# Second attention's query norms computed in its normalising pass, weights turned in the second feed-forward, normalising shared by three engines

## The reference, cut to what matters

```python
def _layernorm(x, axis=-1, eps=1e-05):
    m = jnp.mean(x, axis=axis, keepdims=True)
    v = jnp.var(x, axis=axis, keepdims=True)
    return (x - m) / jnp.sqrt(v + eps)
...
# second attention: H = 16 heads of 8, top_u = 51 of 256 queries per head
Q, K, V = proj(Wq, bq), proj(Wk, bk), proj(Wv, bv)
query_norms = jnp.linalg.norm(Q, axis=2)
_, top_idx = jax.lax.top_k(query_norms, top_u)
Q_sel = jnp.take_along_axis(Q, top_idx[:, :, None], axis=1)
...
x = x + 0.5 * _L0_ffn_ref(_layernorm(x), ...)
x = x + _L0_attn_ref(_layernorm(x), ...)
x = x + 0.5 * _L0_ffn_ref(_layernorm(x), ...)
x = x + 0.5 * _L1_ffn_ref(_layernorm(x), ...)
x = x + _L1_attn_ref(_layernorm(x), ...)
x = x + 0.5 * _L1_ffn_ref(_layernorm(x), ...)
```

## Time and profile before

| | us |
|---|---|
| median of three runs | 1415.3 |
| the profiled execution | 1417.87 |
| its span | 1415.0 |
| busy: PE, DVE, ACT, POOL | 1165.7, 1143.2, 898.3, 695.7 |
| normalising pass before stage 2, first transpose to last copy | 316.65 to 326.13 |
| the same, stage 3, with its statistics | 385.49 to 400.63 |
| second feed-forward | 326.1 to 382.5 |
| second attention: query norms alone | 797.0 to 813.2 |
| second attention: seven rounds | 813.6 to 823.0 |

### The profile page before, as it was taken

How to read it: one execution, slowest core, us unless ns; L and a number is a source line. 1 busy time by engine, 2 the same in 40 slices (tenths; PEclk the granted TensorE clock), 3 DMA queues, 4 the chain that set the end, 5 groups by cost and what they waited for, 6 DMA issues and landing times.

```text
span 1415.0 us, 58469 instructions
## 1 busy us (share of the span) xinstructions
PE 1165.7 (82%) x22908; PEld 956.5 (68%) x22908; DVE 1143.2 (81%) x4087; ACT 898.3 (63%) x2094; POOL 695.7 (49%) x597
## 2 busy tenths in 40 slices
PE   1775898976648899999998759999668999999996
PEld 1563666655527788888888547777437888888886
DVE  4885888857889899999994378888689899999980
ACT  1762566647647878778784426666457687787871
POOL 2305445413037777778775300000058787788772
PEclk9896999987959999999999979999769999999999
DMA  6000000000002222112222000000002121222122
GB/s 167 8 0 1 2 0 0 0 1 1 0 0 48 47 57 46 44 44 46 58 44 48 1 0 1 0 0 0 1 16 53 41 59 44 44 48 56 44 59 78
DMA packets 27515, 42.86 MB, mean 30 GB/s; under 512 B 6960, under 2 KB 18480, under 8 KB 27440
## 3 DMA queue, kind: packets, MB, share of 16 engines
q1 hardware_dynamic: 27440, 41.82, 12.8%
HBM read 6.15 MB, written 2.10 MB: 6 GB/s over the span
## 4 chain that ended last, share of the span: by engine, by line
PE 43%; DVE 23%; ACT 10%; issue 10%; POOL 5%; DMA 4%; SPq 3%; DVEq 1%; ACTq 0%; POOLq 0%; PEldq 0%
PE bank L1715 12%; ACT work L1031 4%; POOL work L345 4%; DVE work L891 4%; DMA rowsD<-work 4%; PE bank L1697 4%; DVE work L934 4%; SPq L315 3%; PE bank L1405 3%; PE bank L1598 2%; DVE xn L565 2%; ACT L1197 2%; PE bank L1688 2%; PE bank L1418 2%; PE bank L1317 2%
## 5 line engine op out<-in xcount | busy, mean ns | idle before, releaser
L1715 PEld LDWEIGHTS bank<-rowsD,work 128*32 128x32 f32 x16384 | 360.6, 195 | 90.4 <-issue 89.7
L1715 PE MATMUL bank<-rowsD,work 128*32 128x32 f32 x16384 | 371.2, 274 | 56.1 <-DMA rowsD<-work 39.6
L422 POOL TENSOR_SCALAR work<-work 128x1024 f32<-128x1024 f32 x64 | 185.2, 2893 | 135.0 <-ACT work L1202 135.0
L409 POOL TENSOR_TENSOR work<-work 128x512 f32<-128x512 f32 x128 | 161.2, 1281 | 41.7 <-ACT work L1230 27.9
L1230 ACT ACTIVATE work<-bank 128x512 f32<-128x512 f32 x128 | 74.9, 612 | 153.8 <-PE bank L1715 150.5
L1202 ACT ACTIVATE work<-work 128x128 f32<-128x128 f32 x512 | 161.1, 405 | 4.1 <-DVE work L954 4.1
L1211 ACT ACTIVATE work<-work 128x128 f32<-128x128 f32 x512 | 160.2, 413 | 0.0
L424 POOL TENSOR_TENSOR work<-work 128x1024 f32<-128x1024 f32 x64 | 157.2, 2456 | 5.3
L934 DVE STREAM_TRANSPOSE work<-work 128x1024 f32<-128x1024 f32 x128 | 151.4, 1222 | 0.0
L1726 PE MATMUL bank<-kout,work 128*128 128x128 f32 x1024 | 128.1, 278 | 3.0 <-POOL work L409 3.0
L1697 PE MATMUL bank<-xT,kinT 128*128 (+1 forms) x512 | 126.6, 392 | 2.6 <-ACT work L1221 2.6
(11 more groups left out here) (196 smaller groups left out, 2285.9 us busy)
## 6 DMA issues: line engine op xcount, KB each, us to landing
rowsD<-work SPq DMA_DIRECT2D x256, 128.0 KB, 2.4
x_sb<-in_L_attn_x_dram SPq DMA_DIRECT2D x8, 256.0 KB, 5.0
out_dram<-x_sb SPq DMA_DIRECT2D x4, 512.0 KB, 5.3
headsel<-in_c_headsel_dram SPq DMA_DIRECT2D x1, 512.0 KB, 5.3
work<-in_L_ffn_key_in_dram SPq DMA_DIRECT2D x1, 512.0 KB, 7.9
kout<-in_L_ffn_key_out_dram SPq DMA_DIRECT2D x4, 128.0 KB, 4.8
work<-in_L_ffn_keys_dram SPq DMA_DIRECT2D x1, 256.0 KB, 2.9
wqkv<-in_L_attn_W_qkv_dram SPq DMA_DIRECT2D x1, 192.0 KB, 5.3
```

The costliest lines, as they stand in the source:

```text
L409: last = nc.gpsimd.tensor_tensor(cg[:, par, :].rearrange("p (j t) -> p j t", j=NCH)[:, :, half * 64:half * 64 + 64], csb[:, par, 512 * hal ...
L422: nc.gpsimd.tensor_scalar(wmask, both, 1.0 - 5e-7, None, ALU.is_ge).then_inc(s["wm"], 1)
L1715: last = nc.tensor.matmul(bank[2 + half][k * NK:(k + 1) * NK, :] .rearrange("p (j t c) -> p t c j", j=NCH, t=16)[:, t % 16, :, :], xrows[: ...
```

## The change

Four edits, made together.

1. **Normalising on three engines.** Of a group's four columns VectorE now writes two, GpSimd the third and ScalarE the fourth, the last as `Identity(scale * x + bias)` with a new tile `shift = negmean * rstd` that VectorE computes first. TensorE waits for all three. GpSimd and ScalarE start when `shift` is written. All loops of the pass are unrolled.
2. **Weights turned in the second feed-forward.** The 16 transposes, the four copies and the 16 small matmuls move from stage 1 into the second feed-forward, one bank at a time: groups 2 to 5 of TensorE's program each take four transposes between project in and project out, groups 6 and 7 eight small matmuls each; VectorE copies a bank after each of its updates 0 to 3. `weff` is copied by ScalarE in the pass of stage 3. The second feed-forward's loops are unrolled.
3. **Query norms inside the pass of stage 4.** After each group's transposes TensorE projects the queries of the group before, 512 tokens at once; ScalarE squares them after its next copy. The sums over heads become 16 matmuls with 32 columns in four column groups, eight for each half of the sequences, into four groups of partitions. Squares of all sequences are kept (`squares`, over `E1` and `PT1`).
4. **Order in the second attention.** VectorE's memsets come before the rounds. GpSimd copies `xs1` for the first sequence before the bias row, and TensorE projects that sequence before the selection is turned.

```diff
             for k in range(STAGES):
-                s = pr
+                s, base = pr, k * NG
+                pool.wait_ge(s["nr"], k + 1)
+                for n in range(NG):
+                    pool.wait_ge(s["tr"], base + n + 1)
+                    pool.sem_inc(s_go, 1)
+                    c = n * GT + 2
+                    nc.gpsimd.tensor_scalar(xn[:, n % 2, 2, :], x_sb[:, c, :], negmean[:, c:c + 1], rstd[:, c:c + 1],
+                                            ALU.add, ALU.mult).then_inc(s["xp"], 1)
                 pool.wait_ge(s["tr"], 2 + (k + 1) * NG)
...
                 if k == 4:
+                    pool.wait_ge(s["ev"], 2 + (k + 1) * NG)
+                    nc.gpsimd.tensor_copy(xs1, xT[:, 0:SEQ]).then_inc(L1["xs"], 1)
                     add_row(bo_bc, L1["cb"])
...
+            def keep_weights(g):
+                dve.wait_ge(s_tw, g + 1)
+                if g == 0:
+                    nc.vector.tensor_copy(w1T[:, :, :].rearrange("p a b -> p (a b)"), bank[0][:, :]).then_inc(s_cw, 1)
+                if g == 1:
+                    nc.vector.tensor_copy(keysT, bank[1][:, :]).then_inc(s_cw, 1)
+                if g > 1:
+                    nc.vector.tensor_copy(kinT[:, :, :, 16 * (g - 2):16 * (g - 1)].rearrange("p j c i -> p i c j"),
+                                          bank[g - 2][:, :].rearrange("p (i c j) -> p i c j", c=4, j=NCH)).then_inc(s_cw, 1)
...
+                nc.vector.tensor_tensor(shift[:, :], negmean[:, :], rstd[:, :], ALU.mult).then_inc(s["nr"], 1)
...
-                    for t in range(GT):
+                    for t in range(2):
                         c = n * GT + t
...
+                else:
+                    for g in range(NG - 2):
+                        sums(g + 1, (g + 1) % 2)
+                        update(g, g % 2)
+                        if g < 4:
+                            keep_weights(g)
...
-                with act.Fori(0, NG // 2) as i:
-                    for par in range(2):
-                        n = 2 * i + par
-                        act.wait_ge(s["tr"], base + n + 3)
-                        nc.scalar.activation(xT[:, bass.ds(n * GW, GW)], bank[6 + par][:, :],
-                                             ACT.Copy).then_inc(s["ev"], 1)
+
+                def normalise(n):
+                    act.wait_ge(s["tr"], base + n + 1)
+                    act.sem_inc(s_go, 1)
+                    c = n * GT + 3
+                    nc.scalar.activation(xn[:, n % 2, 3, :], x_sb[:, c, :], ACT.Identity, bias=shift[:, c:c + 1],
+                                         scale=rstd[:, c:c + 1]).then_inc(s["xa"], 1)
+
+                def evacuate(n):
+                    act.wait_ge(s["tr"], base + n + 3)
+                    nc.scalar.activation(xT[:, n * GW:(n + 1) * GW], bank[6 + n % 2][:, :],
+                                         ACT.Copy).then_inc(s["ev"], 1)
+
+                def query_squares(n):
+                    act.wait_ge(L1["pq"], n + 1)
+                    nc.scalar.activation(squares[n // 4][:, 2 * n % 8:2 * n % 8 + 2, :].rearrange("p a b -> p (a b)"),
+                                         bank[n % 2][:, :], ACT.Square, bias=bqc[:, 0:1]).then_inc(L1["psq"], 1)
+
+                act.wait_ge(s["nr"], k + 1)
+                normalise(0)
+                normalise(1)
+                for n in range(NG):
+                    evacuate(n)
+                    if n + 2 < NG:
+                        normalise(n + 2)
+                    if k == 4 and n > 0:
+                        query_squares(n - 1)
+                    if k == 3 and n == 0:
+                        act.wait_ge(s_tw, 5)
+                        nc.scalar.activation(weff[:, :], bank[0][:, :], ACT.Copy).then_inc(s_cw, 1)
+                if k == 4:
+                    query_squares(NG - 1)
...
-            def turn_weights():
-                pe.wait_ge(s_w, 16 * NW)
+            def turn_weights(g):
+                if g == 0:
+                    pe.wait_ge(s_w, 16 * NW)
+                if g > 1:
+                    pe.wait_ge(s_cw, g - 1)
                 for i in range(4):
-                    c = slice(i * P, (i + 1) * P)
-                    nc.tensor.transpose(bank[1][:, c], w1nat[:, i, :], ident[:, :])
-                    nc.tensor.transpose(bank[2][:, c], keysn[:, i, :], ident[:, :])
-                    nc.tensor.transpose(bank[3][:, c], kinn[:, i, :], ident[:, :])
-                    last = nc.tensor.transpose(bank[4][:, c], kinn[:, 4 + i, :], ident[:, :])
-                last.then_inc(s_ps, 1)
-
-            def fold_keys():
-
-                pe.wait_ge(s_set, SET_KEYS)
+                    src = (w1nat[:, i, :], keysn[:, i, :], kinn[:, i, :], kinn[:, 4 + i, :])[g]
+                    last = nc.tensor.transpose(bank[g % 2][:, i * P:(i + 1) * P], src, ident[:, :])
+                last.then_inc(s_tw, 1)
+
+            def fold_keys(g):
+                if g == 0:
+                    pe.wait_ge(s_cw, 3)
...
-                        last = nc.tensor.matmul(bank[5][:, c * NK:(c + 1) * NK], wqn[:, c, :], kv[:, q, h, :],
-                                                start=True, stop=True)
-                last.then_inc(s_ps, 1)
-                pe.wait_ge(s_set, SET_ALL)
+                for c in range(4 * g, 4 * g + 4):
+                    last = nc.tensor.matmul(bank[0][:, c * NK:(c + 1) * NK], wqn[:, c, :], kv[:, c // PH, c % PH, :],
+                                            start=True, stop=True)
+                if g == 3:
+                    last.then_inc(s_tw, 1)
+
+            def query_squares(n):
+                if n == 5:
+                    head_norms(0)
+                pe.wait_ge(pr["ev"], 2 + 4 * NG + n + 1)
+                if n >= 2:
+                    pe.wait_ge(L1["psq"], n - 1)
+                nc.tensor.matmul(bank[n % 2][:, :], w1T[:, 0, :], xT[:, n * GW:(n + 1) * GW], start=True,
+                                 stop=True).then_inc(L1["pq"], 1)
+
+            def head_norms(half):
+                pe.wait_ge(L1["psq"], 4 * half + 4)
+                for odd in range(2):
+                    for g in range(4):
+                        last = nc.tensor.matmul(bank[2 + half][32 * g:32 * (g + 1), 0:SEQ], headsel[:, odd, 0:32],
+                                                squares[half][:, 2 * g + odd, :], start=(odd == 0), stop=(odd == 1))
+                last.then_inc(L1["pn"], 1)
 
...
+                    pe.sem_inc(s_go, 1)
+                    for t in range(GT):
+                        last = nc.tensor.transpose(bank[6 + n % 2][:, t * P:(t + 1) * P], xn[:, n % 2, t, :],
+                                                   ident[:, :])
+                    last.then_inc(s["tr"], 1)
+                    if k == 4 and n > 0:
+                        query_squares(n - 1)
+                if k == 4:
+                    query_squares(NG - 1)
+                    head_norms(1)
                 pe.wait_ge(s["ev"], 2 + (k + 1) * NG)
 
...
+                        project_in(2 * i, 0)
+                        project_out(2 * i - 1, 1)
+                        project_in(2 * i + 1, 1)
+                        project_out(2 * i, 0)
+                else:
+                    for g in range(2, NG):
+                        project_in(g, g % 2)
+                        if g < 6:
+                            turn_weights(g - 2)
+                        else:
+                            fold_keys(2 * g - 12)
+                            fold_keys(2 * g - 11)
+                        project_out(g - 1, 1 - g % 2)
                 project_out(NG - 1, 1)
...
-                pe.wait_ge(s_set, SET_W1T)
-                for half in range(2):
-                    for b in range(8):
-                        n = half * 8 + b
-                        par = n % 2
-                        if n >= 2:
-                            pe.wait_ge(s["psq"], n - 1)
-                        nc.tensor.matmul(bank[par][:, 0:SEQ], w1T[:, 0, :], xT[:, n * SEQ:(n + 1) * SEQ],
-                                         start=True, stop=True).then_inc(s["pq"], 1)
-                        if b >= 1:
-                            pe.wait_ge(s["psq"], n)
-                            nc.tensor.matmul(bank[2 + half][:, 0:SEQ], headsel[:, b - 1, :], sq1[:, 1 - par, :],
-                                             start=(b == 1), stop=False).then_inc(s["sq_used"], 1)
-                    pe.wait_ge(s["psq"], half * 8 + 8)
-                    nc.tensor.matmul(bank[2 + half][:, 0:SEQ], headsel[:, 7, :], sq1[:, 1, :], start=False,
-                                     stop=True).then_inc(s["sq_used"], 1)
-                    pe.wait_ge(s["sq_used"], 2 + half * 8 + 8)
-                    pe.sem_inc(s["pn"], 1)
-                pe.wait_ge(s["selT"], 2)
-                for c in range(2):
...
+                project(0)
```

107 lines of the change are left out of this document (41 added, 66 removed).

## The result

| | us |
|---|---|
| changed kernel, median of five runs | 1404.42 (1401.72 to 1407.97) |
| kernel before, five runs beside them | 1415.33 (1413.8 to 1417.49) |
| ratio, 95% interval | 0.992, 0.990 to 0.994 |
| forecast, range | 1401.4, 1391 to 1411 |
| profiled execution: before, forecast, measured | 1417.87, 1404.0, 1402.47 |

Faster by 10.9 us on the medians, where 13.9 was forecast: clear of noise, though only 0.8%. The profiled executions differ by 15.4. (In the prediction, "rows 8" is the table by source line and "rows 9" the row at 1004.87 of the second attention's end.)

The account below looks back on a forecast made before the run. No engine was taken to bound the kernel alone, so each stage was read for itself. 2.0 + 3.9 - 0.9 + 8.9 = 13.9 us saved takes the median from 1415.3 to 1401.4 us, range 1391 to 1411.

Parts of the forecast that it names:

- Stage 4: Query norms inside stage 4's pass, with the new start and order: 8.9 us saved, between near nothing and 10.7.
- the 1.45 a group that I gave ScalarE: Stage 4's pass: ScalarE paces with copy, tile and 512-column square, 1.45 us a group at full clock.
- Plain passes: Passes without statistics, tiles on three engines: 0.7 us saved in each, 2.0 in three (0.8 to 3.0).
- the start: From the reciprocal's end to a pass's first transpose: 0.65 to 0.85 us instead of 1.21, 0.4 saved.
- Passes with statistics: Stages 3 and 5: two-group loop 3.13 instead of 3.64 us; 3.9 saved together (2.5 to 5.5).
- Second feed-forward: Unrolled, with the weights' transposes, copies and small matmuls moved in: 0.9 us lost, between nothing and 10.5.
- its cover is complete: Stage 1: GpSimd's 9.83 us bias row hides the copies and small matmuls, so moving them out gains nothing.
- VectorE sets the pace there: Second feed-forward before the change: six groups take VectorE 33.7 us, 5.62 each, its own work 5.39.
- GpSimd against VectorE: Rival, normalising passes: GpSimd's tile slows VectorE's two, costing 8.9 us together, 1410.3 us; chance 0.15.
- The rounds too: Rival, stage 4: GpSimd's bias row also slows VectorE's rounds, which end 8.6 us later, 1418.9 us; chance 0.06.
- Full clock in all passes: Rival: TensorE's four transposes take 0.66 us instead of 1.12 in all passes, 9.2 us more saved, 1392.2; chance 0.12.
- The feed-forward in series: Rival, second feed-forward: all the moved work adds up in series, 10.5 us lost instead of 0.9, 1411.0; chance 0.10.

Follow-up runs that it names:

- the filler in its rounds: Ten unused 128 x 512 TensorE matmuls during stage 4's rounds, added to the three-buffer kernel (1386.42 us): 1385.98 us, ratio 0.9773.
- W: Changed kernel with the weights' transposes, copies and small matmuls back in stage 1, second feed-forward still unrolled: 1399.72 us, ratio 0.9891.

## Why the prediction was right, and where not

**Stage 4, 8.9 forecast, 8.6 and 8.7 measured, 7.8 by undoing edit 3.** The mechanism was right: the norms' own phase of 16.2 us is gone, and 6.5 us (3.4 in the pass, 3.1 behind it) do its work. The sizes within it were partly luck, and they differ between two executions of one program. In the first the stretch up to the second copy is 15.84 us, 1.5 shorter than forecast, because TensorE and ScalarE pipeline better than the 1.45 a group that I gave ScalarE (1.30) and about one group was slow. In the second it is 16.99, with three groups' transposes at 1.2 GHz (1.08, 1.06 and 1.06). From the last row of `max` to the first exponential the first takes 20.05 us and the second 18.76, where it was 19.04 before. The sum comes out the same. The timeline of the first execution there:

```profile
814.73 1.06 PE L1580 MATMUL bank<-work 128*128 128x256 f32 x2
...
819.96 1.93 PE L1592 MATMUL bank<-work 128*32 128x256 f32 x16 [4.17 <-DVE work L783]
821.83 2.08 PE L1562 MATMUL bank<-w1T,work 128*128 128x256 f32 x4
...
823.70 1.06 PE L1565 MATMUL bank<-xT,w1T 128*128 128x256 f32 x2
```

And of the second:

```profile
822.14 1.93 PE L1592 MATMUL bank<-work 128*32 128x256 f32 x16 [4.17 <-DVE work L783]
...
825.82 0.59 PE L1565 MATMUL bank<-xT,w1T 128*128 128x256 f32 x2
```

Before, the first sequence's projections stood between the ranks and the first gather; in them TensorE rose to 2.4 GHz (two matmuls of the second in 0.60), and the gather took 1.56 us behind a pause of 2.32. Now they stand in front of the rounds, TensorE pauses 4.17 and the gather takes 1.93, in both executions and in every kernel of the experiments, which all keep edit 4. It begins 0.34 us sooner after the rounds and ends where it ended before, so edit 4 gave nothing of the 0.2 forecast for it. What differs between the two executions comes behind the gather: in one TensorE goes on at 1.2 GHz for some 3 us more (1.06), in the other it is at 2.4 from there (0.59). What decides between them no run here shows.

**Plain passes, 2.0 forecast, 0.9 and 1.9 measured.** One step failed, the start: "First transpose after 0.65 to 0.85: 0.4 saved." None of it came. The tiles' lengths were near (ScalarE 0.48 for 0.40, GpSimd 0.45 to 0.60 for 0.57 at most). Left out were most of the ways between them: 0.38 us from the reciprocal's start to `shift`, 0.19 for it, 0.24 until GpSimd begins, and 0.2 to 0.3 from its end to TensorE. With GpSimd's tile of 0.5 they take as long as VectorE's own way to four tiles did (1.57 and 1.56). That the loop hardly gains, and why (ScalarE's copy comes onto it), was right and is confirmed by taking ScalarE's tile away: the plain passes get 0.6 to 0.9 us shorter.

That the second execution nearly reaches the forecast is luck. In its stages 0 and 1 TensorE went to 2.4 GHz from the fifth group on, and those passes took 10.30 and 10.20 us instead of 10.87 and 10.84. Two rows of stage 1's pass show it, eight transposes and then four:

```profile
100.28 1.96 PE L1368 MATMUL bank<-ident,xn 128*128 128x128 f32 x8 [0.36 <-ACT xn L1039]
102.58 0.63 PE L1368 MATMUL bank<-ident,xn 128*128 128x128 f32 x4 [0.35 <-ACT xn L1039]
```

The four other plain passes of the two profiles gained 0.15 to 0.41 us each, where 0.7 was forecast.

**Passes with statistics, 3.9 forecast, 4.2 measured.** The loop is 3.10 as forecast at 3.13. The 0.4 for the start, counted in both passes, didn't come; in its place the first loop gave more than the later ones (from the second group's transposes to the fourth's 3.33 us in stage 5 and 3.58 in stage 3, 4.23 before). The copy of `weff` cost 0.1 where 0.5 was taken: the pass of stage 3 is 13.95 us, that of stage 5, without it, 13.81.

**Second feed-forward, 0.9 forecast, 0.9 and 1.8 measured.** The sum was near for a wrong pair of terms. An unrolled group takes 5.42, not 5.15. In the rows from 364.69 on VectorE's instructions follow each other without a wait, so 5.42 is its own work, and the 5.39 that the prediction read as such was the shorter of two spacings (the other is 5.95, 348.44 to 354.39). ScalarE, busy 32.24 of the 33.71 us of the six groups of before, lies just under it. The four copies, 3.4 us long, cost 2.4. What the prediction missed is the comparison that mattered: unrolling without the copies gives 0.7, so the edit as a whole is 4.2 slower on the medians than leaving the weights where they were hidden. I had both halves in hand ("its cover is complete", "VectorE sets the pace there") and never set the one against the other.

**The rivals.** GpSimd against VectorE: refuted, with the 342 ns median beside GpSimd's tile. The rounds too: refuted by 428 ns at most, and 8.8 us from first to last `max` against 8.6. The Trainium skill, "GPSIMD Engine Reference", § 8 Key points, names contention for VectorE instructions in a two-port mode or with two SBUF inputs. For the short tiles beside GpSimd's `tensor_scalar` the trace shows none. For the feed-forward, beside GpSimd's 128 x 512 addition of the bias row, the trace of before agrees with it:

```profile
332.43 5.06 POOL L331 TENSOR_TENSOR x_sb<-x_sb,ffn_add 128x512 f32 x3
...
336.28 1.49 DVE L587 TENSOR_SCALAR work<-work,w2c 128x512 f32<-128x512 f32 x1
...
344.91 0.47 DVE L587 TENSOR_SCALAR work<-work,w2c 128x512 f32<-128x512 f32 x1
```

All four `tensor_scalar` of line 587 that overlap the addition are long (0.669, 1.440, 1.490 and 1.492 us) and the twelve others take 0.469 to 0.489. The ten `scalar_tensor_tensor` of line 591, which have two SBUF inputs, take 1.147 to 1.646 beside it and 0.750 to 0.754 without. The ten `max` beside the same kind of addition in the changed kernel take 409 to 428 ns, the four others 407 to 416. So whether a rival of this kind holds depends on both instructions. Which of the two, GpSimd's instruction or the size of the tile, spares the pass's tiles isn't separated. Full clock in all passes: did not happen, 0.50 in stage 3's window as before; in the second execution it came for half of two plain passes and gave about 0.6 us in each. The feed-forward in series: groups of 6.03 to 6.29 us instead of more than 7, refuted, and TensorE's share by itself costs 0.4.

**The median.** 12.8 to 13.1 us left the changed stretches of the profiles and 10.9 to 11.5 the medians. The difference is within what the first attention's stretch varies by from profile to profile (up to 2.9 us over all kernels here, 1.4 for one program), and I can't assign it further.

## What to carry to other kernels

When a loop goes through several engines, more engines on its work shorten it little; what does is a buffer more and a written order in which no engine stands behind the hand-off that it waits for. Here that gave 13.3 us on top of what was left of the change, where sharing the same tiles among three engines had given 3.7, and with it sharing is worth 9.8. When an instruction is moved, ask also whether it kept TensorE's clock up where it was: edit 4 began the gather 0.34 us sooner and made it 0.37 longer. Read a stretch of a few microseconds in more than one profile before you give it a cause: the same program took 20.05 and 18.76 us here between the same two instructions. Before work is moved out of a stage, look at what ends that stage: work under a complete cover is already free, and the place it goes to seldom is. The best kernel is the one with three buffers, the norms in the pass and the weights back in stage 1, 1386.42 us, 2.1% below the kernel before (ratio 0.9789, 0.9771 to 0.9808); the filler in its rounds makes no measurable difference.

## What the runs showed of the hardware

- GpSimd's first tile starts 0.24 us after VectorE's `shift` ends and ScalarE's 0.15 after it, and TensorE follows GpSimd by 0.2. With tiles of half a microsecond such hand-offs are as large as the work.
- An `Identity` activation with per-partition scale and bias takes 0.48 to 0.49 us for 128 x 128; an exponential of 128 x 128 with a bias alone (line 1202 of before) takes 0.40 on the median; a 128 x 512 square with bias takes 0.69, the plain copy 0.60.
- VectorE's 128 x 128 tiles beside GpSimd's `tensor_scalar` are slowed from 349 to 404 ns at most, the median not at all. Beside GpSimd's 128 x 512 addition a 128 x 512 `tensor_scalar` went from 0.47 to 0.49 us up to 1.49 and a `scalar_tensor_tensor` from 0.75 up to 1.65, while `max` stayed as it was.
- The granted clock in stage 3's pass was 0.50 with two buffers and 0.83 with three. It did little for the loop: with three buffers groups of transposes stand 0.85 us apart at 1.2 GHz and 0.87 at 2.4 in the plain passes, and 1.10 to 1.11 at either in stages 3 and 5. What is left for the clock is the end of stages 3 and 5, 0.5 us each (1.26 us from the last group's first transpose to the end of the pass, 1.73 in W). So some 12 of the 13.3 us are the loop's: groups of 0.86 and 1.11 us, where 0.95 and 1.2 were expected.
